# A router's gates split between two engines, the second norm's scale moved into them, and the expert biases added in float32

## The reference, cut to what matters

```
def _ln_t(v, eps=1e-05):
    m = mean(v, axis=-1); s = var(v, axis=-1)
    return (v - m) / sqrt(s + eps)

def _L1_ffn_ref(x, router_w, router_b, expert_w, expert_b):
    router_probs = softmax(x @ router_w + router_b)
    top_p, top_i = top_k(router_probs, 2)
    top_p = top_p / sum(top_p)
    expert_out = einsum('bnd,edc->bnec', x, expert_w) + expert_b
    gathered = take_along_axis(expert_out, top_i)
    return einsum('bnk,bnkc->bnc', top_p, gathered)

t = t + _L1_ffn_ref(_ln_t(t), router_w, router_b, expert_w, expert_b)
```

## Time and profile before

| | us |
|---|---|
| median of 3 runs | 246.77 |
| lowest, highest | 244.46, 251.44 |
| span of the profiled execution | 242.4 |

### The profile page before, as it was taken

The page is one execution under the profiler, slowest core; times in us unless marked ns, Lnnn a source line. Parts: engine busy times, 40 slices in busy tenths (PEclk is TensorE's granted clock), DMA queues, the critical chain, the costliest instruction groups (busy, mean ns, idle before and its releaser), DMA issues.

```text
span 242.4 us, 6269 instructions
## 1 busy us (share of the span) xinstructions
PE 232.0 (96%) x2389; PEld 127.4 (53%) x2390; DVE 199.9 (82%) x423; ACT 174.9 (72%) x361; POOL 45.4 (19%) x81
## 2 busy tenths in 40 slices
PE   8899999999999999999999999999999998889894
PEld 6355454555555555555555555555444685558421
DVE  2999798999999999999999999999722683349773
ACT  3544738998999989989899988998996332329710
POOL 6974079300000002000000320000200000000250
PEclk9999999999999999999999999999999999999999
DMA  5005600161131221442300000000000000000002
GB/s 141 0 28 203 124 3 3 33 226 26 54 91 45 49 58 33 103 133 87 96 8 0 4 3 3 4 0 4 4 0 4 0 0 3 3 0 0 4 0 87
DMA packets 6082, 10.09 MB, mean 42 GB/s; under 512 B 2236, under 2 KB 3820, under 8 KB 5924
## 3 DMA queue, kind: packets, MB, share of 16 engines
q1 hardware_dynamic: 5908, 9.63, 13.6%
q10 hardware_dynamic: 144, 0.07, 0.1%
HBM read 6.84 MB, written 2.62 MB: 39 GB/s over the span
## 4 chain that ended last, share of the span: by engine, by line
PE 53%; DVE 2%; issue 1%; ACT 0%; DVEq 0%
PE psum L592 15%; PE psum L529 10%; PE psum L493 6%; PE psum L630 4%; PE psum L910 3%; PE psum L562 2%; PE psum L819 1%; PE psum L809 1%; PE psum L798 1%; PE psum L846 1%; PE psum L857 1%; PE psum L891 1%; PE psum L644 1%; PE psum L838 1%; PE psum L753 1%
## 5 line engine op out<-in xcount | busy, mean ns | idle before, releaser
L1301 DVE TENSOR_REDUCE half_max<-psum 128x1 f32<-128x512 f32 x256 | 157.2, 682 | 4.5 <-PE psum L493 3.8
L1116 ACT ACTIVATE probs<-psum 128x512 f32<-128x512 f32 x228 | 120.2, 605 | 13.9 <-PE psum L529 11.3
L493 PE MATMUL psum<-kop,qop 64*128 64x512 f32 x256 | 87.0, 439 | 0.7 <-DVE kop L1265 0.6
L529 PE MATMUL psum<-qop,kop 64*128 64x512 f32 x256 | 83.8, 440 | 0.5 <-ACT qop L1121 0.4
L592 PE MATMUL psum<-probs,v_aug 128*32 128x256 f32 (+1 forms) x1296 | 73.1, 341 | 0.2 <-DVE o_sb L1315 0.2
L529 PEld LDWEIGHTS psum<-qop,kop 64*128 64x128 f32 x256 | 39.5, 184 | 21.6 <-ACT probs L1116 10.7
L592 PEld LDWEIGHTS psum<-probs,v_aug 128*32 128x32 f32 x1296 | 32.3, 109 | 32.4 <-issue 22.1
L493 PEld LDWEIGHTS psum<-kop,qop 64*128 64x128 f32 x256 | 40.5, 184 | 16.7 <-DVE half_max L1301 9.2
L1009 POOL CAST max_part<-negmax 128x8 fp32r<-128x8 f32 x13 | 2.5, 190 | 97.1 <-issue 85.3
L1050 POOL TENSOR_TENSOR early<-probs,early 128x512 f32<-128x512 f32 x4 | 5.1, 1273 | 57.1 <-ACT probs L1211 56.9
L1112 ACT ACTIVATE probs<-psum 128x1024 f32<-128x1024 f32 x14 | 13.4, 1028 | 0.3
(11 more groups left out here) (191 smaller groups left out, 196.9 us busy)
## 6 DMA issues: line engine op xcount, KB each, us to landing
parts_scratch<-early SPq DMA_DIRECT2D x4, 512.0 KB, 3.8
qop<-parts_scratch SPq DMA_DIRECT2D x28, 64.0 KB
vt_sb<-in_vt SPq DMA_DIRECT2D x1, 1024.0 KB, 4.8
kop<-parts_scratch SPq DMA_DIRECT2D x14, 64.0 KB
kop<-parts_scratch SPq DMA_DIRECT2D x28, 32.0 KB
x_sb<-in_x SPq DMA_DIRECT2D x2, 256.0 KB, 3.5
q_pair<-in_q_pairs SPq DMA_DIRECT2D x1, 512.0 KB, 3.4
qop<-max_row SPq DMA_DIRECT2D x26, 4.0 KB
```

The lines of the kernel that those rows point to most:

```text
L493: last = nc.tensor.matmul(psum[:, m % MAX_BANKS, :], qop[at, b * PP + pp, qh * NH + t * P:qh * NH + (t + 1) * P], kop[at, b * PP + pp, c * ...
L529: last = nc.tensor.matmul(psum[:, bank, :], kop[at, b * PP + pp, mt * P:(mt + 1) * P], qop[at, b * PP + pp, qh * NH:(qh + 1) * NH], start= ...
L1116: last = nc.scalar.activation(probs[:, n % P_RING, h, :], psum[:, bank, :], ACT.Exp, scale=SCALE)
L1301: V.tensor_reduce(half_max[:, i, c, h * HT + t:h * HT + t + 1], psum[:, m % MAX_BANKS, :], AX_X, ALU.max, negate=True).then_inc(S["slot_fr ...
```

## The change

Only the last stage and its preparations differ. Up to the last `cen2` product every engine has the same instructions in the same order, but for three things on GpSimd and SP: GpSimd no longer zeroes all of `expb_sb` and no longer splits the biases; in block 11 it zeroes `bias_gates` (128x256) and copies `centre` twice into `cen_dup` (64x128 each); SP issues 8 small loads there, not 12.

- **Tokens in channels.** `y`, its 16 ScalarE instructions and 16 transposes go. Four float32 products of `cen_dup` (K = 64, M = 128) by `t2` (512 columns) give the centred, unscaled tokens in channels at once. ScalarE copies them to `yt2` as before, and its exponential stands between the second and the third copy.
- **Scale in the gates.** `share` = reciprocal x `rstd`, and `gates_s` = gates x `share` is what is split.
- **Gates.** VectorE ends the first half of the tokens alone; GpSimd does the last 7 steps of the second half, and two more that give the unscaled gates `bias_gates`.
- **Biases.** TensorE transposes `bias_gates` (4 float32 transposes to 64 rows), ScalarE copies them out, and two float32 products with K = 16 add the biases, in the middle of the second half. The experts' own products open the sums.
- **Shares and order.** GpSimd multiplies jobs 5 and 7 only, VectorE 14 of 16. TensorE's order is written out anew, 8 spreads ahead of the first experts. Both halves' gate transposes use bank 2. One `keep_warm(34)` stands behind the logits, none later. The first output piece is written behind the last multiplication.

```diff
...
-GT_BANKS = (2, 5)
+GT_BANK = 2
-BY_POOL = [i for i in range(B, len(MOE) - B) if i % 3 == 2]
+BY_POOL = [5, 7]
+GATE_ROWS = 32
...
-y = spare_q[:, 0:2 * N].rearrange("p (t b u c) -> p t b u c", t=TT, b=B, u=2)
+bias_t = spare_q[0:HALVES * GATE_ROWS, 0:NH]
...
-keep_warm(44, YT_BANKS[3])
+pe.wait_ge(S["cen_dup_ready"], 2)
 for c in range(2):
-    if c:
-        keep_warm(10, YT_BANKS[3])
-    pe.wait_ge(S["y_ready"], TT * B // 2 * (c + 1))
     for b in range(B):
-        for t in range(4 * c, 4 * c + 4):
-            last = nc.tensor.transpose(psum[:, YT_BANKS[2 * c + b], (t % 4) * P:(t % 4 + 1) * P],
-                                       y[:, t, b, :, :], ident)
-        last.then_inc(S["yt_full"], 1)
-keep_warm(3, GB_BANKS[0])
-pe.wait_ge(S["logits_read"], 1)
-for c in range(2):
-    pe.wait_ge(S["gate_split"], c + 1)
+        nc.tensor.matmul(psum[:, YT_BANKS[2 * c + b], :], cen_dup[image(b), :, :].rearrange("p u c -> p (u c)"),
+                         t2[image(b), c * NH:(c + 1) * NH], start=True, stop=True).then_inc(S["yt_full"], 1)
+pe.wait_ge(S["logits_read"], 2)
+keep_warm(34, GB_BANKS[0])
+def gates_to_rows(c):
     for t in range(TT // 2):
-        last = nc.tensor.transpose(psum[:, GT_BANKS[c], t * P // 2:(t + 1) * P // 2].bitcast(BF16),
+        last = nc.tensor.transpose(psum[:, GT_BANK, t * P // 2:(t + 1) * P // 2].bitcast(BF16),
                                    gate_part[:, c * TT // 2 + t, :], ident_bf)
     last.then_inc(S["gt_full"], 1)
+def bias_gates_to_rows():
+    pe.wait_ge(S["gates_ready"], 2)
+    pe.wait_ge(S["gt1_ready"], 1)
+    for t in range(TT // 2):
+        last = nc.tensor.transpose(psum[0:HALVES * GATE_ROWS, GT_BANK, t * P:(t + 1) * P], bias_gates[:, t, :], ident)
+    last.then_inc(S["bias_t_full"], 1)
+pe.wait_ge(S["gate_split"], 1)
+gates_to_rows(0)
 pe.wait_ge(S["gt0_ready"], 1)
...
-    if i < len(GB_BANKS) and GB_BANKS[i] == GT_BANKS[1]:
-        pe.wait_ge(S["gt1_ready"], 1)
     if i == len(MOE) // 2:
         pe.wait_ge(S["gt1_ready"], 1)
+    if i >= len(GB_BANKS) and GB_BANKS[i % len(GB_BANKS)] == GT_BANK:
+        pe.wait_ge(S["bias_t_ready"], 1)
     r = i - len(GB_BANKS)
     if r in BY_DVE:
         pe.wait_ge(S["scaled_dve"], BY_DVE.index(r) + 1)
...
     nc.tensor.matmul(psum[:, GB_BANKS[i % len(GB_BANKS)], :], select[rows, k, :],
                      gate_t[rows, c * NH:(c + 1) * NH], start=True, stop=True).then_inc(S["gb_full"], 1)
-def expert_bias(c):
-    for s in range(3):
-        nc.tensor.matmul(psum[:, MOE_BANKS[c], :], expb_part[:, s, :],
-                         gate_t[:, c * NH:(c + 1) * NH], start=s == 0, stop=False,
-                         skip_group_check=True)
-def experts(first):
...
+def expert_biases():
+    pe.wait_ge(S["bias_t_ready"], 1)
+    for c in range(HALVES):
+        at = slice(c * GATE_ROWS, c * GATE_ROWS + B * E)
+        nc.tensor.matmul(psum[:, MOE_BANKS[c], :], expb_sb[at, :], bias_t[at, :], start=False, stop=False,
+                         skip_group_check=True).then_inc(S["bias_done"], 1)
+def experts(first, end):
+    for pair in range(first, end, B):
+        for r in range(pair, pair + B):
+            if r in BY_DVE:
+                pe.wait_ge(S["scaled_dve"], BY_DVE.index(r) + 1)
+            else:
+                pe.wait_ge(S["scaled_pool"], BY_POOL.index(r) + 1)
+        for r in range(pair, pair + B):
+            c, b, k = MOE[r]
+            if k == 0 and b == 0:
+                pe.wait_ge(S["yt_ready"], c + 1)
+            nc.tensor.matmul(psum[b * C:(b + 1) * C, MOE_BANKS[c], :], expw_sb[:, k, :],
+                             scaled[:, r % SCALED, :], start=k == 0, stop=False,
+                             skip_group_check=True).then_inc(S["moe_done"], 1)
 def broadcasts(first, end):
-    for i in range(first, end):
-        gate_bank_free(i)
-    for i in range(first, end):
-        gates_over_rows(i)
-broadcasts(0, 4)
-expert_bias(0)
-broadcasts(4, SCALED)
-for first in range(0, len(MOE), B):
-    if first == len(MOE) // 2:
-        expert_bias(1)
-    experts(first)
-    broadcasts(first + SCALED, min(first + SCALED + B, len(MOE)))
+    for pair in range(first, end, B):
+        for i in range(pair, pair + B):
+            gate_bank_free(i)
+        for i in range(pair, pair + B):
+            gates_over_rows(i)
+broadcasts(0, 8)
+pe.wait_ge(S["gate_split1"], 1)
+pe.wait_ge(S["gb_copied"], BY_POOL.index(len(GB_BANKS) - 1) + 1)
+gates_to_rows(1)
+experts(0, 4)
+bias_gates_to_rows()
+broadcasts(8, 10)
+experts(4, 8)
+broadcasts(10, 16)
+experts(8, 10)
+expert_biases()
+experts(10, 16)
...
+            nc.gpsimd.tensor_copy(cen_dup[at, :, :], centre[at, at].rearrange("p (o c) -> p o c", o=1)
+                                  .broadcast_to([C, 2, C])).then_inc(S["cen_dup_ready"], 1)
...
+G = nc.gpsimd
+pool.wait_ge(S["late_hot"], 1)
+pool.wait_ge(S["exp2_ready"], 1)
+link(G.tensor_tensor(late(hot2), late(hot2), each(ed), ALU.mult))
+link(G.tensor_tensor(late(gates), late(hot1), late(hot2), ALU.add))
+pool.wait_ge(S["share_ready"], 3)
+link(G.tensor_tensor(late(gates_s), late(gates), each(share), ALU.mult))
+link(G.tensor_copy(gp(0), tiles(gates_s)))
+link(G.tensor_tensor(tiles(gate_rest), tiles(gates_s), gp(0), ALU.subtract))
+link(G.tensor_copy(gp(1), tiles(gate_rest)))
+G.tensor_tensor(gp(2), tiles(gate_rest), gp(1), ALU.subtract).then_inc(S["gate_split1"], 1)
+pool.wait_ge(S["mixed"], 1)
+for c in range(HALVES):
+    at = slice(c * TT * B // 2, (c + 1) * TT * B // 2)
+    G.tensor_tensor(bias_gates[:, :, c * GATE_ROWS:c * GATE_ROWS + B * E].rearrange("p t (b e) -> p t b e", b=B),
+                    gates[:, at, :].rearrange("p (t b) e -> p t b e", b=B),
+                    gate1[:, at].rearrange("p (t b o) -> p t b o", b=B, o=1).broadcast_to([P, TT // 2, B, E]),
+                    ALU.mult).then_inc(S["gates_ready"], 1)
...
-act.wait_ge(S["logits_read"], 1)
-for t in range(TT):
-    if t == TT - 3:
-        act.wait_ge(S["delta_ready"], 1)
-        nc.scalar.activation(ed[:], dlt[:], ACT.Exp).then_inc(S["exp2_ready"], 1)
-    for b in range(B):
-        nc.scalar.activation(y[:, t, b, :, :],
-                             cen2[:, t:t + 1, b * C:(b + 1) * C].broadcast_to([P, 2, C]), ACT.Copy,
-                             scale=rstd[:, t * B + b:t * B + b + 1]).then_inc(S["y_ready"], 1)
-for i in range(4):
+def channels(i):
     c, b = divmod(i, 2)
     act.wait_ge(S["yt_full"], i + 1)
     nc.scalar.activation(yt2[:, b, c * NH:(c + 1) * NH], psum[:, YT_BANKS[i], :],
                          ACT.Copy).then_inc(S["yt_ready"], 1)
-act.wait_ge(S["gt_full"], 2)
-nc.scalar.activation(gate_t[:, NH:], psum[:, GT_BANKS[1], 0:NH // 2].bitcast(BF16),
-                     ACT.Copy).then_inc(S["gt1_ready"], 1)
-for n, i in enumerate(BY_POOL):
+def gates_aside(n):
+    i = BY_POOL[n]
     act.wait_ge(S["gb_full"], i + 1)
-    if n >= 2:
-        act.wait_ge(S["scaled_pool"], n - 1)
     nc.scalar.activation(gate_copy[:, n % 2, :], psum[:, GB_BANKS[i % len(GB_BANKS)], :],
                          ACT.Copy).then_inc(S["gb_copied"], 1)
+channels(0)
+channels(1)
+act.wait_ge(S["delta_ready"], 1)
+nc.scalar.activation(ed[:], dlt[:], ACT.Exp).then_inc(S["exp2_ready"], 1)
+channels(2)
+channels(3)
+gates_aside(0)
+gates_aside(1)
+act.wait_ge(S["gt_full"], 2)
+nc.scalar.activation(gate_t[:, NH:], psum[:, GT_BANK, 0:NH // 2].bitcast(BF16),
+                     ACT.Copy).then_inc(S["gt1_ready"], 1)
+act.wait_ge(S["bias_t_full"], 1)
+nc.scalar.activation(bias_t, psum[0:HALVES * GATE_ROWS, GT_BANK, :], ACT.Copy).then_inc(S["bias_t_ready"], 1)
...
+dve.wait_ge(S["dve_chain"], chain[0] - 1)
+chain[0] += 1
+V.tensor_tensor(of(hot2), over_tokens(weight_sb), over_e(pick), ALU.is_equal).then_inc(S["dve_chain"], 1)
+dve.wait_ge(S["dve_chain"], chain[0] - 1)
+V.tensor_tensor(hot2[:, G8:, :], over_tokens(weight_sb), to_e(pick, slice(G8, 2 * G8)), ALU.is_equal).then_inc(S["late_hot"], 1)
 dve.wait_ge(S["exp2_ready"], 1)
 V.tensor_scalar(gate1[:], ed[:], 1.0, None, ALU.add).then_inc(S["share_ready"], 1)
-one_hot(hot2)
+dve.wait_ge(S["dve_chain"], chain[0])
+chain[0] += 1
+V.tensor_tensor(of(hot2), of(hot2), over_e(ed), ALU.mult).then_inc(S["dve_chain"], 1)
 dve.wait_ge(S["share_ready"], 1)
 V.reciprocal(gate1[:], gate1[:]).then_inc(S["share_ready"], 1)
-halves(lambda c: V.tensor_tensor(of(hot2, c), of(hot2, c), over_e(ed, c), ALU.mult))
-halves(lambda c: V.tensor_tensor(of(gates, c), of(hot1, c), of(hot2, c), ALU.add))
+dve.wait_ge(S["dve_chain"], chain[0])
+V.tensor_tensor(of(gates), of(hot1), of(hot2), ALU.add).then_inc(S["mixed"], 1)
 dve.wait_ge(S["share_ready"], 2)
-halves(lambda c: V.tensor_tensor(of(gates, c), of(gates, c), over_e(gate1, c), ALU.mult))
+V.tensor_tensor(share[:], gate1[:], rstd[:], ALU.mult).then_inc(S["share_ready"], 1)
+dve.wait_ge(S["mixed"], 1)
+dve.wait_ge(S["share_ready"], 3)
+link(V.tensor_tensor(of(gates_s), of(gates), over_e(share), ALU.mult))
...
+link(V.tensor_copy(gp(0), by_tile(gates_s)))
```

(42 more changed lines are left out.)

82 lines of the change are left out of this document (39 added, 43 removed).

## The result

| | before | changed |
|---|---|---|
| median of 12 runs, us | 245.74 | 247.92 |
| lowest, highest | 244.24, 251.44 | 246.76, 248.81 |
| span of the profiled execution | 242.4 | 246.0 |

What follows compares the result with a forecast made beforehand. The end was taken to be set by when the gates are in rows and TensorE's work behind VectorE's first two multiplications: -0.72, 0.60 given back, then 10.40 against 10.25, net +0.03 on 246.77, so 246.8 us; range 244.4 to 249.6.

Steps and rivals of the forecast that it cites:

- Range and class: Whole kernel: 244.4 to 249.6 us, and a time within 2% of the kernel before, chance 0.90.
- the point: Whole kernel: 246.8 us, from the 246.77 median of three runs and a span change of +0.03 us.
- TensorE's clock falls and comes back: Last stage: sparse TensorE work halves its clock for a while, +1.7 to +2.5 us, about 248.9; chance 0.12.
- the forecast's overlap of TensorE's idle stretches with VectorE's work at no price: Last stage: TensorE idles at 224.1 to 225.7 and 227.2 to 228.3 us, with later products at full rate.
- the stretch: TensorE between 224.1 and 228.3 us: only 0.24 + 0.75 us of work, which might lower its clock.
- Work ahead of the gates: Up to the first spreads: gate transposes begin at 225.69 instead of 226.41, first spreads at 226.44 instead of 227.16; -0.72 us.
- rival 2: Gate steps: GpSimd working on SBUF beside VectorE slows VectorE's steps, +1.3 us, 248.1; chance 0.15.
- VectorE's own steps: First half's gates on VectorE: dependent steps from the second place at 223.55 take 2.1 us, ready at 225.65.
- Behind the first spreads: First spreads to first experts' products: two more spreads and four transposes give back 0.60 of the 0.72 us gained.
- TensorE's list: TensorE from the first experts' products to the end: removed, moved and added products sum to 10.40 us against 10.25.
- hidden as stated: Last stage: VectorE's multiplications have 0.5 us slack and GpSimd's seven gate steps 2.0, so neither delays the end.
- Sum: Last stage's end: 228.90 + 10.40 = 239.30 us against 239.27, so +0.03.

Runs made afterwards that it cites:

- the first edit: Changed kernel with the padding behind the logits lengthened from 34 to 50 products, nothing else; last stage 24.90 us, 246.59 us in its one run.
- The tokens part alone: Kernel before with only the tokens in channels by four products, the reciprocal root in the gates and 48 padding products; last stage 23.95 us against 24.27.
- four variants with one filling: Changed kernel with 50 padding products, alone, with GpSimd kept apart or all gates on VectorE; or with only the two later fillings. Stages 24.90, 24.57, 26.56, 24.90 us.

## Why the prediction was right and wrong

- **Range and class: right**, 247.92 in 244.4 to 249.6 and within 2%. The sum behind the point, 246.8, was not. The point came within 1.1 us of the time partly by luck: it stood on the 246.77 of three runs, and twelve runs have 245.74, so that the change was +2.2 where I had +0.03.
- **The clock.** The rival "TensorE's clock falls and comes back", with 0.12, is what happened. The step that failed is the forecast's overlap of TensorE's idle stretches with VectorE's work at no price: its sum has every product behind them at full rate. I had counted the stretch (1.0 us of work between 224.1 and 228.3) and its price as +1.7 to +2.5; it was 27.29 - 24.90 = 2.39. That the price fits is partly luck: I had the clock low for 3.4 to 4.9 us, and it was low for 6.8; less than half of that was lost, since TensorE waited for VectorE in a part of it (0.61 us ahead of 229.20). I gave the case 0.12 because no row of the trace showed it; the padding, 57 products whose results nobody reads, was a sign that I did not follow up. The Trainium skill (TensorE: Matmul & The Clock Gate, Part 1) has an idle array fall to half rate; the kernel without padding agrees, where the clock was 0.50 behind 4.85 us of idling. In the changed kernel it fell with no idle stretch above 1.89 us.
- **Work ahead of the gates: mis-sized.** With the clock held, the first spreads come 11.26 after the stage's start, not 10.66 as I had it (226.44 - 215.78). Of the 0.60, 0.33 is GpSimd's interference, shown by keeping it apart: my rival 2, at a quarter of its 1.3. VectorE's own steps were right: kept apart, its parts end 9.90 after the stage's start (228.71 - 218.81), predicted 9.87 (9.82 if the terms are added rightly: they make 2.05, not 2.1). Most of the rest is a row that I read wrongly. The chain's 0.24 for the four transposes counts from the end of the padding, 226.41; in the timeline of the same execution they start at 226.25 and end at 226.65, 0.40 later. Behind gates that are only just ready all of it counts: 0.41 in the changed kernel's chain.
- **Behind the first spreads: right.** 2.51 to the experts, predicted 2.46. Before it was 1.86, so 0.65 was given back here, predicted 0.60. But of the 0.72 to be gained ahead of it only 0.12 came.
- **TensorE's list: right within 0.2.** With the clock held by the first edit it took 10.22 from the first experts' product to the last (10.40), bias transposes 0.56 to 0.63 with their switch (0.60), bias products 1.06 side by side (1.01). VectorE and GpSimd were hidden as stated.
- **Sum.** At full clock the change costs 24.90 - 24.27 = +0.63 rather than +0.03 (first spreads -0.12, from there to the experts +0.65, TensorE's list +0.02, last product to last addition +0.08), at its own clock +3.02. The medians differ by 2.2, less than the profiled spans' 3.6. A part of the kernel before's runs lose time to a low clock elsewhere (below), while the mean clocks of the changed kernel's twelve runs leave room for the one drop with cost only. That this is all of the difference was not shown.

Where did the part gains go? The tokens part alone is worth -0.3. What came with it, GpSimd's half of the gates and more steps ahead of the experts, costs 0.95 (0.21 of it ahead of the first spreads, 0.65 from there to the experts). And the idling left behind by the products that were taken away costs 2.4. Whether the drop comes from the work of one stretch or also from when it falls was not settled: of five kernels with nearly the same stage, the changed one has the mean clock of a drop in twelve of twelve runs, and of four variants with one filling one dropped in its profiled execution and three did not.

## What to carry to other kernels

When a change takes products away from an engine whose clock follows its work, count the idle stretches that it opens, just ahead of the work that sets the end, and fill all of them (one filling held the clock in three kernels and not in a fourth), best with work that has to be done anyway: the bias products cost 1.06 us behind the experts' start and nothing in the wait ahead of it. Splitting a chain of short dependent steps between two engines has little to win where each step's two halves already overlap, and the second engine can take it back: the first spreads came at 11.27 without the split, 11.26 with it, and 10.93 with it and the engines kept apart.
